# Router logits by column strips of TensorE, the first convolution ahead of the second counts, and half of the zeros ahead of the weights

## What is computed

```python
xf = xn.reshape(t, d)                                   # t = 4096, d = 128
probs = softmax(xf @ Wr)                                # Wr is 128 x 8
eidx = argmax(probs); p_tok = probs[eidx]
rank = (how many earlier tokens chose the same expert)
keep = rank < 512                                       # capacity 512 rows for each expert
xe = xf[dispatch]                                       # gather, 8 x 512 rows
y  = relu(xe @ W1) @ W2                                 # 128 -> 512 -> 128, per expert
y * p_tok, scattered back to the tokens' rows
```

## Time and profile before

| | us |
|---|---|
| three runs | 130.11, 130.77, 130.87 (median 130.77) |
| span of the profiled execution | 128.8 |
| median less that span | 2.0 |
| busy PE, DVE, ACT, POOL | 106.2, 101.8, 99.6, 84.6 |

### The profile page before, as it was taken

One profiled execution on the slowest core, in us unless ns is written; L12 is line 12 of the kernel. 1 busy time (PEld: TensorE's weight loads), 2 busy tenths in 40 slices (PEclk: granted clock), 3 DMA queues, 4 the chain that ended last, 5 costly groups with the idle time before them and its releaser, 6 DMA issues.

```text
span 128.8 us, 2229 instructions
## 1 busy us (share of the span) xinstructions
PE 106.2 (82%) x711; PEld 89.9 (70%) x711; DVE 101.8 (79%) x238; ACT 99.6 (77%) x219; POOL 84.6 (66%) x109
## 2 busy tenths in 40 slices
PE   3999999999799999999999997999997999700000
PEld 3999976672379779789879987898697899600000
DVE  5398998999699999979614489999999975973690
ACT  3299792888589589789689999999999799823560
POOL 8987774078788787778777877888787878700000
PEclk9999999999999999999999999999999999998555
DMA  2966964892456365312611711111110111149995
GB/s 85 383 247 173 405 244 173 318 380 66 103 169 181 80 209 139 118 53 56 209 41 41 219 51 41 61 37 41 52 57 25 60 43 61 41 108 302 325 372 215
DMA packets 8234, 19.27 MB, mean 150 GB/s; under 512 B 1689, under 2 KB 1945, under 8 KB 8224
## 3 DMA queue, kind: packets, MB, share of 16 engines
q1 hardware_dynamic: 5424, 13.70, 31.5%
q0 software_dynamic: 2080, 4.19, 11.2%
q10 hardware_dynamic: 720, 1.25, 2.6%
HBM read 10.82 MB, written 8.39 MB: 149 GB/s over the span
## 4 chain that ended last, share of the span: by engine, by line
PE 60%; DVE 9%; DMA 8%; ACT 8%; issue 5%; POOL 4%; POOLq 1%; SPq 1%; DVEq 0%; ACTq 0%
PE bank L624 17%; PE bank L609 6%; PE bank L611 6%; PE bank L610 6%; DMA dec<-y_rows 4%; PE bank L640 4%; PE bank L453 3%; PE bank L561 3%; PE bank L442 3%; POOL xn_tok L405 3%; DMA xn_tok<-xn_rows,idx_in 2%; ACT xc L796 2%; PE bank L594 2%; PE bank L563 2%; PE bank L562 2%
## 5 line engine op out<-in xcount | busy, mean ns | idle before, releaser
L405 POOL DMA_INDIRECT xn_tok<-xn_rows,idx_in x32 | 33.7, 1054 | 14.4 <-issue 9.4
L417 POOL DMA_INDIRECT y_rows<-xn_tok,idx_out x32 | 33.5, 1047 | 9.7 <-issue 9.1
L624 PE MATMUL bank<-w_raw,h_sb 128*128 128x128 f32 x256 | 29.9, 275 | 0.0
L624 PEld LDWEIGHTS bank<-w_raw,h_sb 128*128 128x128 f32 x256 | 29.2, 192 | 0.0
L786 ACT ACTIVATE h_sb<-bank 128x512 f32<-128x512 f32 x32 | 18.8, 598 | 2.5 <-PE bank L611 0.6
L609 PE MATMUL bank<-xg_hi,w_hi 128*128 128x512 f32 x32 | 13.2, 412 | 0.0
L611 PE MATMUL bank<-xg_hi,w_lo 128*128 128x512 f32 x32 | 12.6, 393 | 0.0
L610 PE MATMUL bank<-xg_lo,w_hi 128*128 128x512 f32 x32 | 12.5, 391 | 0.0
L1021 DVE SCALAR_TENSOR_TENSOR xc<-xnT,par,xc 128x1020 f32<-128x1020 f32 (+2 forms) x9 | 11.5, 1277 | 0.3
L640 PE MATMUL bank<-par,xc 128*128 128x128 f32 x64 | 8.8, 280 | 2.2 <-ACT xc L796 1.3
L1061 DVE TENSOR_TENSOR_SCAN xnT<-dec,bank 128x256 f32<-128x256 f32 x16 | 10.1, 674 | 0.3
(11 more groups left out here) (143 smaller groups left out, 243.2 us busy)
## 6 DMA issues: line engine op xcount, KB each, us to landing
w_raw<-in_weights SPq DMA_DIRECT2D x8, 512.0 KB, 3.9
y_rows<-sca SPq DMA_DIRECT2D x4, 512.0 KB, 5.9
dec<-y_rows SPq DMA_DIRECT2D x8, 256.0 KB, 5.7
x_tok<-in_x SPq DMA_DIRECT2D x3, 512.0 KB, 5.9
xn_rows<-xn_tok SPq DMA_DIRECT2D x3, 512.0 KB, 3.6
out<-dec SPq DMA_DIRECT2D x4, 256.0 KB, 3.1
out<-dec ACTq DMA_DIRECT2D x4, 256.0 KB, 2.9
x_tok<-in_x SPq DMA_DIRECT2D x2, 256.0 KB, 3.5
```

The source lines that it names most:

```text
L405: g.indirect_dma_start(gathered[:, s * D:(s + 1) * D], None, xn_rows, bass.IndirectOffsetOnAxis(ap=idx_in[:, s:s + 1], axis=0)).then_inc(g ...
L417: g.indirect_dma_start(y_rows, bass.IndirectOffsetOnAxis(ap=idx_out[:, s:s + 1], axis=0), gathered[:, s * D:(s + 1) * D], None, bounds_che ...
L624: last = mm(tile_of(e, s), h_sb[:, k * CAP + s * P:k * CAP + (s + 1) * P], w_raw[:, e, F + k * D:F + (k + 1) * D], start=(k == 0), stop=(k ...
```

## The change

The router's matmul is turned round. For a half h the weights are now `w_router` with 32 columns (8 wanted), and 512 columns of `xT` are the moving side. Four such matmuls, for the four groups of the half, write to the four strips of 32 partitions of one PSUM bank, each with its own strip of 32 columns of the array (`tile_position=(0, 32*j)`). ACT copies the bank to SBUF (`keep_logits`), and four transposes on PE (`by_token`) give the logits by token in the same bank. So 32 router matmuls of 128 columns are replaced by 8 of 512, 8 transposes and 2 copies.

Other edits: PE's order is written out anew, `counts(0)` comes after `router(1)`, `conv(0)` runs in one piece ahead of `counts(1)`, and the table is built in five parts after it, with ACT's copy of the totals (`totals_done`) awaited by the first. DVE takes all statistics ahead of `marks(0)`, and the comparison `lows(8)` stands behind `marks(1)`. The shift `nmr` is made by two small instructions on POOL for each eight tiles, not by one on DVE. ACT normalises 13 tiles instead of 17 and POOL 19 instead of 15. `values` is filled by POOL (a quarter), ACT (two quarters) and DVE (one) from a row `count16`. The idle matmuls at the start are five, not seven. On SP the zeros 0 and 1 come behind x and behind the second store, the weights of expert 0 behind the third store, those of expert 1 behind the last, then `gam` and the zeros 2 and 3.

```diff
-        POOL_TILES = (2, 3, 6, 7, 10, 11, 14, 15, 18, 19, 22, 23, 26, 27, 30)
-        ACT_TILES = (0, 1, 4, 5, 8, 9, 12, 13, 16, 17, 20, 21, 24, 25, 28, 29, 31)
+        ACT_TILES = (3, 7, 11, 15, 19, 22, 23, 26, 27, 28, 29, 30, 31)
+        POOL_TILES = tuple(t for t in range(NT) if t not in ACT_TILES)
...
-            first_weights(0)
+            sp.wait_ge(zeroed, 1)
+            clear(0)
             for u, (t0, nt) in enumerate(UNITS):
                 normalised(sp, (t0 + nt) // 4 - 1)
                 sp.dma_start(own_rows(xn_rows, t0, nt), tiles(xn_tok, t0, nt)).then_inc(xn_out, 16)
+                if u == 1:
+                    clear(1)
                 if u == 2:
-                    first_weights(1)
+                    first_weights(0)
+            first_weights(1)
             sp.dma_start(gam[:, :], gamma.partition_broadcast(P)).then_inc(gam_in, 16)
+            clear(2)
+            clear(3)
...
+            def inverse(q):
+                cols = slice(q * QT, (q + 1) * QT)
+                pool.wait_ge(stat_done, (q + 1) * QT // 2)
+                g.tensor_scalar(nmr[:, cols], stats[:, cols, 1], -1.0, None, ALU.mult).then_inc(minus_done, 1)
+                pool.wait_ge(minus_done, q + 1)
+                pool.wait_ge(rstd_done, q + 1)
+                g.tensor_tensor(nmr[:, cols], nmr[:, cols], rstd[:, cols], ALU.mult).then_inc(nmr_done, 1)
...
-            for _ in range(7):
+            for _ in range(5):
                 mm(bank[7][:, 0:P], ident[:, :], ident[:, :], start=True, stop=True)
...
+            def router(h):
+                if h == 0:
                     pe.wait_ge(router_w, 1)
+                transposed(pe, 4 * h + 3)
+                for j in range(P // STRIP):
+                    n = 4 * h + j
+                    last = mm(strips[h][j * STRIP:(j + 1) * STRIP, :], w_router[:, :], xT[:, n * HT:(n + 1) * HT],
+                              start=True, stop=True, tile_position=(0, j * STRIP))
+                last.then_inc(strips_done, 1)
+
+            def by_token(h):
+                pe.wait_ge(logitsT_done, h + 1)
+                for i in range(4):
+                    last = nc.tensor.transpose(strips[h][:, i * P:(i + 1) * P],
+                                               logitsT[h][:, i * P:(i + 1) * P], ident[:, :])
                 last.then_inc(logits_done, 1)
...
+            for n in range(1, 5):
+                turned(n)
+            router(0)
+            turned(5)
+            by_token(0)
+            turned(6)
             columns_of(0)
-            router(NH - 1)
+            turned(7)
+            columns_of(1)
+            router(1)
+            counts(0)
+            columns_of(2)
+            by_token(1)
+            columns_of(3)
...
-            for n in range(1, 3):
-                columns_of(n)
-            conv(0, 0, 2)
+            conv(0, 0, TAPS)
             counts(1)
...
-            table_of(0)
-            columns_of(3)
-            conv(0, 2, 3)
-            table_of(1)
-            conv(0, 3, TAPS)
-            for n in range(4, NH):
-                columns_of(n)
+            columns_of(4)
+            table_of(0)
+            table_of(8)
+            columns_of(5)
+            table_of(16)
+            table_of(22)
+            table_of(28)
+            columns_of(6)
+            columns_of(7)
             conv(1, 0, TAPS)
...
             untile(0)
             untile(1)
+            root(0)
+            untile(2)
+            untile(3)
             root(1)
+            untile(4)
+            root(2)
+            keep_logits(0)
+            untile(5)
             normalise(0)
-            untile(2)
+            root(3)
+            untile(6)
             normalise(1)
-            root(2)
-            untile(3)
+            untile(7)
+            keep_columns(0)
             normalise(2)
-            untile(4)
+            keep_logits(1)
             normalise(3)
...
             marks(0)
             inverse(3)
-            moments(4)
             ranks(0)
-            inverse(4)
             places(0)
+            lows(0)
             marks(1)
+            lows(8)
             ranks(1)
             places(1)
-            dve.wait_ge(before_done, NP + 1)
+            lows(16)
+            lows(22)
+            lows(28)
+            dve.wait_ge(totals_done, 1)
```

More of the change, by code:

```diff
@@ L154, in rglru_moe_kernel @@
         xn_bank = [bank[4], bank[5], bank[0]]
-        centred = bank[7][:, 0:P]
+        centred = bank[7][:, 0:STRIP]
         gate = [bank[4], bank[5]]
@@ L159, in rglru_moe_kernel @@
         tb = bank[6]
-        logits = [bank[6][:, 0:PT * E], bank[2][:, 0:PT * E]]
-        table = bank[3][:, 0:NS]
-        before = [bank[7][:, 0:E * PT], bank[6][:, 2 * E * PT:3 * E * PT]]
-        totals = bank[7][:, E * NT:E * NT + E]
+        strips = [bank[6], bank[2]]
+        table = bank[7][:, 0:NS]
+        before = [bank[3][:, 0:E * PT], bank[3][:, E * PT:2 * E * PT]]
+        counted = bank[7][:, E * NT:E * NT + E]
         obank = [bank[4], bank[5], bank[7]]
@@ L474, in counts, with table_of @@
                    stop=True).then_inc(before_done, 1)
-            def table_of(h):
-                pe.wait_ge(hi_done, h + 1)
-                for t in range(h * PT, (h + 1) * PT):
-                    if t in LOW_STARTS:
-                        pe.wait_ge(low_done, LOW_STARTS.index(t) + 1)
-                    last = mm(table, low_eq[:, :, t], hi_val[:, h, :, :, t - h * PT].rearrange("p e s -> p (e s)"),
+            def table_of(t0):
+                t1 = (LOW_STARTS + (NT,))[LOW_STARTS.index(t0) + 1]
+                pe.wait_ge(hi_done, t0 // PT + 1)
+                pe.wait_ge(low_done, LOW_STARTS.index(t0) + 1)
+                if t0 == 0:
+                    pe.wait_ge(totals_done, 1)
+                for t in range(t0, t1):
+                    last = mm(table, low_eq[:, :, t],
+                              hi_val[:, t // PT, :, :, t % PT].rearrange("p e s -> p (e s)"),
                               start=(t == 0), stop=(t == NT - 1))
-                if h == NP - 1:
+                if t1 == NT:
                     last.then_inc(table_done, 1)
@@ L675, in _, with root @@
             nc.scalar.preload_act_table_set("sqrt_and_others")
[L677 to L679 removed]
+            def root(q):
+                cols = slice(q * QT, (q + 1) * QT)
+                if q == 0:
                     act.wait_ge(eps_done, 3)
[L681 to L683 removed]
+                act.wait_ge(stat_done, (q + 1) * QT // 2)
+                a(std[:, cols], stats[:, cols, 2], ACT.Sqrt, bias=eps[:, 0:1], scale=1.0 / D).then_inc(std_done, 1)
             def normalise(n):
[L686 removed]
+                act.wait_ge(nmr_done, n // 2 + 1)
                 for t in range(4 * n, 4 * n + 4):
@@ L910, in per_token, with by_group, by_group_of @@
                 return ap.unsqueeze(2).to_broadcast([P, n, E])
-            lg = [part.rearrange("p (t e) -> p t e", e=E) for part in logits]
+            def by_group(ap):
+                return ap.rearrange("p (j i) -> p j i", i=RUN)
+            def by_group_of(ap):
+                return ap.rearrange("p (j i) e -> p j i e", i=RUN)
+            lg = [part[:, :].rearrange("p (i j w) -> p j i w", i=RUN, w=STRIP)[:, :, :, 0:E] for part in strips]
             number = [0] * NP
```

179 lines of the change are left out of this document (89 added, 90 removed).

## The result

The changed kernel takes 129.31 us (median of four runs, 128.43 to 130.86), the kernel before 130.82 beside it on the same chip: a ratio of 0.9861, with a 95% interval of 0.9818 to 0.9905. Between the medians lie 1.5 us. The profiled execution took 129.72, with a span of 128.0. Ratios leave disturbed runs out, so one may differ from that of two medians.

The account below looks back on a forecast made before the run. PE and POOL were taken as full after the front, so only an earlier first gather, bound by the indices, helps. Span 128.8 - 1.5 = 127.3, plus 2.0 around it, gave 129.3 us; range 128.6 to 132.5, the forecast's own 128.7 to 129.8.

Parts of the forecast that it names:

- The price of the new router: PE's router: a half's four strips run side by side, 0.86 plus 0.2 for staggered starts, 1.05 us.
- passes one behind another: Rival, PE's strips: in-order starts make a half cost 2.15 us; indices 0.5 late, time 131.2; chance 0.24.
- strips in series: Rival, PE's strips: four in a row take 3.44 us a half; indices 3.1 late, time 133.9; chance 0.12.
- marks(0): DVE's first-half marks, after x, statistics and logits: start at 11.2 us, from 11.83.
- The rest, 3.83: DVE from ranks(1) to idx_in: the same work as before, 3.83 us, putting idx_in at 23.4.
- gain at the indices 1.5: End of DVE's front: idx_in moves from 24.91 to 23.4 us, a gain of 1.5.
- The stores: Stores of xn: last issued at 19.7 us, landing at 23.1, before the first gather's need at about 24.
- the stores bind: Rival, SP's queue: zeros and weights ahead make the last store up to 1.5 us late; 129.5 to 130.8; chance 0.10.
- Edits that I cost at nothing: `values`, weights and zeros: all arrive before need; weights 1 near 25 us, costing only if 3 us later.
- From there every row 1.5 earlier: Profile sign: from PE's first gathered rows, at 31.7 us, every row comes 1.5 us earlier.
- The gather waits for `idx_out`: Profile sign on POOL: the first gather, at 24.4 us, waits for `idx_out` and not for a DMA.
- The clock: Rival, PE's start: fewer idle matmuls keep the low clock; until 14 us, indices 1.4 late, time 132.2; chance 0.14.

Follow-up runs that it names:

- a_counts_first: Changed kernel with PE's counts of the first half ahead of the second half's strips; 129.89 us, ratio 0.994 to the kernel before, profiled execution 132.04.
- a_split_stores: Changed kernel, counts first, first convolution cut in two, tile 22 moved to POOL, zeros 2 and 3 after expert 0's gather; 130.45 us, ratio 0.996.
- a_strips_twice: Changed kernel with every router strip matmul issued twice, same result; 133.16 us, ratio 1.015 to the kernel before.
- a_sp_old: Changed kernel with SP's DMAs in the old order, all four writes of zeros last; 130.14 us, ratio 0.995 to the kernel before, profiled execution 133.25.
- a_split_fill: As a_split_stores, plus four idle 128 by 128 matmuls ahead of the first gate; 130.77 us, ratio 0.997 to the kernel before.
- a_again: The changed kernel run once more, unedited, giving its second profile; 129.38 us, ratio 0.987 to the kernel before.
- a_zeros_wait: Changed kernel with zeros 2 and 3 held back until the weights of expert 1 have landed; 129.37 us, ratio 0.988 to the kernel before.
- a_split: Changed kernel with first-half counts ahead of the second strips and the first convolution cut in two, half behind the table; 130.12 us, ratio 0.988.
- b_sp_new: The kernel before with only SP's DMAs in the new order; 130.59 us, ratio 1.000 to the kernel before.
- after: The changed kernel itself, in its first measurement and profile, against the kernel before; 129.31 us, ratio 0.986.
- a_conv_later: Changed kernel with PE's first convolution moved behind the counts of the second half; 133.38 us, ratio 1.026 to the kernel before.
- a_later_fill: As a_conv_later, plus eight idle 128 by 128 matmuls between the first gate's matmul and turning the gathered rows; 133.49 us, ratio 1.013.

## Why the prediction was right, and where not

The time (129.3 forecast, 129.31 measured) and its main mechanism held: the strips run side by side, the indices come earlier, and the rest moves with the gather. That the number fits to 0.01 is luck. The indices gained less than forecast and x landed later; the gather's last DMA and what lies around the span made up for it, which the sum had taken as unchanged.

- *The price of the new router, 1.05 a half*: 1.06 to 1.07 by the modelled ends, 1.00 from start to start. The parts were not those of the sum: the four strips start within 0.02 us of one another, not 0.06 apart each. The rival of passes one behind another (2.15) and that of strips in series (3.44) are false. The Trainium skill, "TensorE: Matmul & The Clock Gate", Part 3, gave 1.1 to 1.2 by my estimate from its figure for three strips; the trace is a little better. Its rule that matmuls start and end in the order of the program, read as I read it for that rival, does not hold for the two records of strips in different columns: by it a half would have cost 2.15.
- *marks(0), 11.2 with x at 9.40*: 11.68 with x at 9.88, exact from x. *ranks(0), 14.5*: 15.15, 0.17 over from x. *marks(1)*: 17.62, where 17.23 was due from x, since places and comparison took 2.47, not 2.25. *ranks(1)*: 20.35 for 20.03. *The rest, 3.83*: 4.04, beside PE's table in more parts. *idx_in, 23.4*: 24.39, of which x is 0.48 and these terms 0.5. So the step "gain at the indices 1.5" was mis-sized: it measured 1.0 from x (0.76 in the second profile). `conv(0)` ended about when DVE's scan did, as forecast; a_counts_first, which shortened one wait alone, gained nothing.
- *The stores*: issued as forecast (20.29 with x 0.48 later), but landing took 4.4 in the first profile, not 3.4. They landed at about 24.7, 0.7 ahead of the gather. POOL was to end its tiles at 17.6 and ended at 19.4 and, in the second profile, at 20.1, barely ahead of ACT; that is why it had nothing to give in a_split_stores. The rival *the stores bind* did not happen, but was one edit away: it did in a_strips_twice, a_sp_old, a_split_stores and a_split_fill.
- *Edits that I cost at nothing* is the step that failed. Weights 1 were to land near 25 and landed at 28.5 and 26.9. The sentence "if they landed 3 us later they would cost" came true in the first profile (PE's wait of 1.46 at 31.58): it cost 0.3 there, since the gather was hardly earlier, and 1.5 in the profile of a_counts_first, where they landed at 29.0. And the order of SP's DMAs, which I had as free, is worth about 1 us in this kernel if the two ratios are taken at their word. What exactly it buys in a median execution was not shown.
- *From there every row 1.5 earlier*: the last scatter is 0.6 earlier in either profile of the changed kernel, 1.1 to 1.3 from x. The spans fell by 0.8 and 1.2, since the end behind the last scatter was 0.2 and 0.5 shorter too. What lies around the span was 1.7 in the runs of the changed kernel and 2.0 in the median of those before; I don't know why, and 0.3 of the gain is there.
- *The gather waits for `idx_out`*: so the profile names it, but by the program it waits for `idx_in`. The sum was not touched by it.
- *The clock*: the start was slower, but off the path. With two idle matmuls fewer ahead the first transposes ran at the low rate (four in 0.91, from 4.47 to 5.38, where they take 0.44), and the strips at 9.20 ran at the full one. No run shows whether it was those two. In the profile of a_counts_first the low rate lasted to 8.9 and the first logits were waited for, so that rival is not dead. The clock fell again from 24 to 27, off the path (`conv(1)` still ended before the gather landed in a_again). Its real price, unforeseen, is in the five traces with holes of 2.5 to 3.8 us ahead of PE's rows: 0.7 to 2.1 us between rows and last scatter. That this is the clock's is shown for one of them, where 0.9 went away with PE kept busy.
- *Price of the losing rivals*: I gave strips at 2.15 a half 131.2; a_strips_twice with 1.92 took 133.16. I had added the delay of the index chain only (1.2 here). The store added 1.3 ahead of the gather, and 2.1 came behind PE's rows, with the clock at 0.50 from 34 to 41.

No kernel tried beats the changed one; a_zeros_wait and a_split equal it.

## What to carry to other kernels

Narrow outputs of a small matmul can go to separate column strips, and four of them cost little more than one (1.00 against 0.86 us here); but look first at what is queued behind them on the same engine, for the new order without the fast strips was a loss. Where three arrivals (indices, stores, weights) end within a us, an edit that speeds one shows nothing and an edit that delays one costs more than its delay: look at the next two before taking the sum at its word. Compare profiles from the landing of the input, not from the first instruction, as long as the input is what the chain waits for (in a_counts_first it was not). And where a forecast hits to the digit, compare its terms: here two misses and two unforeseen gains cancelled.

## What the runs showed of the hardware

- Four float32 matmuls of 32 columns in four column strips, two records each, took 1.06 us in all by the modelled ends and 1.00 from start to start; a float32 matmul of 128 columns alone, 0.86. Four records start within 0.02 us, the other four 0.45 later. Twice as many took 1.92.
- The landing of x, with the same DMAs ahead, varied from 9.21 to 10.31 us between the profiles. The 512 KB of weights 1, with a store ahead and zeros behind in the queue, took from 4.6 us (b_sp_new) to 8.0 (a_counts_first) to land, the last 512 KB store of xn from 3.2 (b_sp_new) to 6.1 (a_strips_twice).
- The granted clock fell to 0.50 behind an idle stretch of PE of only 0.43 us, among transposes and small matmuls (after). It stayed at 1.00 behind one of 3.04 (a_conv_later) and was low behind one of 3.02 (a_later_fill), two kernels that are alike up to that place.
